# A graph attention layer on one core: later stores, counting before the unit, and another split of the slots

## The reference

```python
# x: 8192 x 256, adj: 8192 x 8192 f32, sparse: about 16 positive values a row, far more in the
# first rows; H = 8 heads of D = 32; W, Wr: 256 x 256
h0 = relu(layernorm(x))
h = (h0 @ W.T).reshape(n, 8, 32)
s_src, s_dst = einsum(h, a_src), einsum(h, a_dst)            # n x 8 each
attn = s_src[:, None, :] + s_dst[None, :, :] + adj[:, :, None] * We[:, 0] + be
attn = leaky_relu(where(adj[:, :, None] > 0, attn, -inf), 0.2)
attn = softmax(attn, axis=1)
out = x + einsum('ijh,jhd->ihd', attn, h) + h0 @ Wr.T + br
```

## Time and profile before

| | us |
|---|---|
| median of 3 runs | 2901.33 (2899.38 to 2902.26) |
| profiled execution | 2921.01 |
| its span | 2919.2 |
| VectorE busy | 2210.1 (76%) |
| POOL busy | 1471.8 (50%) |
| ScalarE busy | 1270.4 (44%) |
| TensorE busy | 1241.1 (43%) |
| gathers (L491) | 943 + 194, 1137 in all |
| activations that weight (L944) | 4024 |
| stores (L500) | 60 of 63 recorded, mean 1.644 |

### The profile page before, as it was taken

One profiled execution on the slowest core, in us unless ns is written; L12 is line 12 of the kernel. 1 busy time (PEld: TensorE's weight loads), 2 busy tenths in 40 slices (PEclk: granted clock), 3 DMA queues, 4 the chain that ended last, 5 costly groups with the idle time before them and its releaser, 6 DMA issues.

```text
span 2919.2 us, 27617 instructions
## 1 busy us (share of the span) xinstructions
PE 1241.1 (43%) x5305; PEld 934.9 (32%) x5306; DVE 2210.1 (76%) x5479; ACT 1270.4 (44%) x4898; POOL 1471.8 (50%) x1649
## 2 busy tenths in 40 slices
PE   7980040403351245523543351542352352436885
PEld 5650040303241133412332241332241241224664
DVE  3559879399997588668999798897998861129992
ACT  2320021102253278536845552743543563655663
POOL 5763655635736644565457647637537537530000
PEclk9995575756655566556656565656565666567998
DMA  3574647556666556656667668768758724257770
GB/s 119 190 283 147 181 134 222 87 198 168 200 187 195 172 173 177 175 150 208 202 203 233 206 193 231 227 183 228 215 183 229 216 62 98 70 162 165 197 156 3
DMA packets 226531, 512.82 MB, mean 176 GB/s; under 512 B 98280, under 2 KB 116400, under 8 KB 224208
## 3 DMA queue, kind: packets, MB, share of 16 engines
q1 hardware_dynamic: 151280, 319.60, 34.3%
q0 software_dynamic: 74960, 191.61, 26.4%
q10 hardware_dynamic: 144, 0.13, 0.0%
HBM read 475.19 MB, written 36.03 MB: 175 GB/s over the span
## 4 chain that ended last, share of the span: by engine, by line
issue 30%; DVE 22%; DMA 21%; PE 9%; ACT 7%; POOL 5%; another core or an unknown queue 2%; SPq 2%; DVEq 0%; POOLq 0%; ACTq 0%; PEldq 0%
DMA adj_sb<-in_adj_dram 16%; DVE work L617 6%; ACT arena L944 6%; DVE work L613 6%; POOL arena L491 4%; DMA arena<-table,arena 3%; DVE arena L753 2%; PE banks L1055 2%; PE banks L1049 2%; SPq L392 1%; DMA arena<-table,own 1%; PE banks L1098 1%; PE banks L1052 1%; DVE work L649 1%
## 5 line engine op out<-in xcount | busy, mean ns | idle before, releaser
L491 POOL DMA_INDIRECT arena<-table,arena x943 | 958.0, 1016 | 398.2 <-issue 281.2
L1076 PE MATMUL banks<-arena,ident 128*128 128x256 f32 x1268 | 421.0, 507 | 1326.6 <-DVE arena L753 1182.9
L944 ACT ACTIVATE arena<-arena,prob 128x32 f32<-128x32 f32 x4024 | 879.9, 316 | 107.7 <-issue 103.0
L1076 PEld LDWEIGHTS banks<-arena,ident 128*128 128x128 f32 x1268 | 326.0, 263 | 1418.9 <-issue 1080.3
L617 DVE FIND_INDEX8 work<-work,adj_sb 128x8 uint32<-128x176 f32 (+30 forms) x833 | 645.5, 799 | 1.0 <-issue 1.0
L613 DVE MAX8 work<-adj_sb 128x8 f32<-128x176 f32 (+30 forms) x833 | 594.2, 789 | 65.8 <-DMA adj_sb<-in_adj_dram 62.2
L939 ACT ACTIVATE prob<-pre 128x104 f32<-128x104 f32 (+26 forms) x63 | 20.3, 322 | 1058.3 <-DVE pre L737 704.6
L1082 PE MATMUL banks<-arena,ident 128*128 128x256 f32 x1006 | 321.7, 452 | 224.0 <-remote 118.4
L1082 PEld LDWEIGHTS banks<-arena,ident 128*128 128x128 f32 x1006 | 202.4, 218 | 332.3 <-remote 135.3
L491 POOL DMA_INDIRECT arena<-table,own x194 | 204.0, 1052 | 156.1 <-issue 62.9
L500 POOL DMA_INDIRECT out_dram<-w_all,arena x60 | 98.6, 1644 | 281.1 <-DVE w_all L763 220.9
(11 more groups left out here) (140 smaller groups left out, 1882.2 us busy)
## 6 DMA issues: line engine op xcount, KB each, us to landing
adj_sb<-in_adj_dram SPq DMA_DIRECT2D x504, 512.0 KB
arena<-dst_rows SPq DMA_DIRECT2D x16, 2048.0 KB, 8.8
arena<-table,arena POOLq DMA_INDIRECT x943
table<-arena POOLq DMA_DIRECT2D x32, 264.0 KB, 2.9
arena<-in_x_dram SPq DMA_DIRECT2D x32, 256.0 KB, 3.0
resid<-arena POOLq DMA_DIRECT2D x32, 256.0 KB, 2.6
out_dram<-arena POOLq DMA_DIRECT2D x32, 256.0 KB, 2.8
work<-table SPq DMA_DIRECT2D x8, 1024.0 KB, 11.2
```

What stands on the lines that cost most here:

```text
L491: pool.indirect_dma_start(gath[:, un.slot(k), :], None, table[:, :], bass.IndirectOffsetOnAxis(ap=rec[:, k, 0:1], axis=0), bounds_check=N ...
L944: last = s.activation(g, g, ACT.Copy, scale=prob[:, b, k * H + h:k * H + h + 1])
L1076: last = m.matmul(ps_sum[:, u % 2, :], ident[:, :], gath[:, un.slot(k), 0:HD], start=(k == 0), stop=False)
```

## The change

- POOL stores a unit's result six units later instead of three (LATE), for which there are eight output buffers instead of four (OUTS): four where they were, two in a spare part of the work memory, two new ones.
- The ring of gathered slots has 84 slots instead of 86.
- FOUND and LEAD: up to two finds more are done by the end of a unit.
- `act_slots`: a unit of fewer than 24 slots gives ScalarE all but two of them, and at most 13; before it was half of them below 18 slots, 10 for 18 and 19, and 14 for 20 to 23. Other units are as before.
- `placed_at` is gone. In the unit in which a group's last tile is found, all finds are done first, then the group is counted, then come the unit's softmax, weights and evacuation, and then place. TensorE does the group's ranks ahead of the unit's sums instead of behind them.

By the plan the groups are now counted and placed in units 1, 4, 8, 16, 24, 32, 40 and 48 and dealt after 2, 5, 12, 20, 28, 36, 44 and 52; the last find is in unit 48. ScalarE has 667 of the 1137 slots instead of 503: 12 more in units 10 to 15, 115 more in units 16 to 48 and 37 more (71 to 108) in units 49 to 62.

```diff
@@ -35,7 +35,7 @@
 PAD = 8
 JBITS = 17
 LOW = (1 << JBITS) - 1
-GSLOTS = 86
+GSLOTS = 84
 LANES = 4
 PIECES = 8
 PIECE = N // PIECES
@@ -53,16 +53,16 @@
           (56, (20, 13, 11, 10, 9, 8, 7, 6)))
 DIRECT = (75, 61, 58)
 SEGS = {1: (45, 2.2), 2: (30, 1.8), 3: (22, 1.8), 8: (18, 1.6), 14: (14, 1.8), 32: (9, 1.8)}
-FOUND = (4, 7, 10, 12, 15, 16, 18, 20, 21, 22)
-LEAD = 13
+FOUND = (4, 7, 10, 12, 15, 17, 19, 21, 23, 24)
+LEAD = 15
 GMAX = max(len(ks) for _, ks in GROUPS)
 KLIST = max(ks[0] for _, ks in GROUPS)
 KMAX = 8 * (max(DIRECT) // 8 + 1)
 VMAX = 8 * max(n for n, _ in SEGS.values())
 WIDE = max(len(ks) * (HEAD + 2 * ks[0]) for _, ks in GROUPS)
 RANKS = max(len(ks) * (ks[0] + 1) for _, ks in GROUPS)
-OUTS = 4
-LATE = 3
+OUTS = 8
+LATE = 6
 GROUP = 8
 HALF = N // 2
 
@@ -81,7 +81,7 @@
 
     def __init__(self, u, K, source, group, place):
         self.u, self.K, self.source, self.group, self.place = u, K, source, group, place
-        self.act_slots = K // 2 if K < 18 else 10 if K < 20 or K > 38 else 14 if K < 32 else 16
+        self.act_slots = min(K - 2, 13) if K < 24 else 10 if K > 38 else 14 if K < 32 else 16
         self.parts = 2 if K < 30 else 3 if K < 40 else 8
 
     def dve_parts(self):
@@ -122,8 +122,7 @@
     found = [FOUND[u] if u < len(FOUND) else min(len(sources), u + LEAD) for u in range(len(units))]
     for group in groups:
         group.ranked_at = min(u for u in range(len(units)) if found[u] >= group.listed)
-        group.placed_at = min(group.ranked_at + 1, group.first - 2)
-        group.dealt_after = min(max(group.placed_at + 1, group.first - 3), group.first - 1)
+        group.dealt_after = min(max(group.ranked_at + 1, group.first - 3), group.first - 1)
         group.loaded_after = min(group.dealt_after + 1, group.first - 1)
 
     at, owner, part_sums, acts, issued = 0, [None] * GSLOTS, 0, 0, 0
@@ -250,7 +249,9 @@
         rsum = sb("rsum", [P, H])
         rinv = sb("rinv", [P, 2, H])
         w_flat = w_all[:, :, :].rearrange("p c n -> p (c n)")
-        out_sb = w_flat[:, 0:OUTS * HD].rearrange("p (b n) -> p b n", n=HD)
+        out_more = sb("out_more", [P, 2, HD])
+        out_sb = [w_flat[:, i * HD:(i + 1) * HD] for i in range(4)] + [spare(HD) for i in range(2)]
+        out_sb += [out_more[:, i, :] for i in range(2)]
         pad_row = prob[0:PAD, 0, 0:ROW]
 
 
@@ -499,7 +500,7 @@
                 lane = turn(un.store_seq)
                 pool.indirect_dma_start(
                     out[:, :], bass.IndirectOffsetOnAxis(ap=record(un)[:, 0:1].bitcast(U32), axis=0),
-                    out_sb[:, un.u % OUTS, :], None,
+                    out_sb[un.u % OUTS], None,
                     bounds_check=N - 1, oob_is_err=False, compute_op=ALU.add).then_inc(lane, 16)
 
             def deal(group):
@@ -760,18 +761,21 @@
                 dve.wait_ge(S["recip"], u + 1)
                 if u >= OUTS:
                     landed(dve, units[u - OUTS].store_seq + 1)
-                v.tensor_tensor(out_sb[:, u % OUTS, :].rearrange("p (h d) -> p h d", d=D),
+                v.tensor_tensor(out_sb[u % OUTS].rearrange("p (h d) -> p h d", d=D),
                                 ps_sum[:, u % 2, :].rearrange("p (h d) -> p h d", d=D),
                                 rinv[:, u % 2, :].unsqueeze(2).to_broadcast([P, H, D]), ALU.mult).then_inc(S["evac"], 1)
 
             done_finds = 0
             for un in units:
-                while done_finds < found[un.u] - 1:
+                ranked = [group for group in groups if group.ranked_at == un.u]
+                while done_finds < found[un.u] - (not ranked):
                     find(done_finds)
                     for m in range(2 * sources[done_finds].rounds):
                         sort_step(done_finds, m)
                     decode(done_finds)
                     done_finds += 1
+                for group in ranked:
+                    count(group)
                 c = done_finds if done_finds < found[un.u] else None
                 steps = 0 if c is None else 2 * sources[c].rounds
                 if c is not None:
@@ -786,13 +790,8 @@
                     done_finds += 1
                 if un.u:
                     evacuate(units[un.u - 1])
-                for group in groups:
-                    if group.placed_at == un.u > group.ranked_at:
-                        place(group)
-                    if group.ranked_at == un.u:
-                        count(group)
-                        if group.placed_at == un.u:
-                            place(group)
+                for group in ranked:
+                    place(group)
             evacuate(units[-1])
 
             dve.wait_ge(S["fl_t"], 1)
@@ -1101,10 +1100,10 @@
                          ).then_inc(S["rank_ps"], 1)
 
             for un in units:
-                tile_sums(un)
                 for group in groups:
                     if group.ranked_at == un.u:
                         ranks(group)
+                tile_sums(un)
 
             pe.wait_ge(S["over_c"], len(groups))
             pe.wait_ge(S["flag_b"], TILES - FIRST)
```

## The result

The changed kernel takes 3012.15 us (3008.2 to 3013.05, four executions) against 2901.8 us (2899.38 to 2903.96) for the kernel before: a ratio of 1.0378 with a 95% interval of 1.036 to 1.0396. The forecast was 2872 us, its range 2820 to 2940. The changed kernel's profiled execution took 3012.46 us (span 3010.6), 91.5 us more than the 2921.01 of before; that execution of before was itself 19 us above its median.

What follows compares the result with a forecast made beforehand. Bounds taken: VectorE up to 1409 us (fully from 839), chained adjacency pieces to 2351, then ScalarE's weighting. Gains 44 + 50 = 94, losses 28 + 37 = 65, 29 us net: 2901 - 29 = 2872 us, range 2820 to 2940.

Steps and rivals of the forecast that it cites:

- A: Stretch until tile 32's load is issued, 1409 us before: 44 us gained, 94 with X.
- A, group 0's wait: VectorE's wait for TensorE's ranks before group 0's placement in unit 1: it goes, 45.2 us gained.
- A, the other placements and the finds: Up to tile 32's load: new rank waits lose 9 us, finds gain 8, slots gain 3, finds before softmax lose 3.
- X: VectorE's late short operations, 839 to 1409 us: 50 us gained of 126 idle; range 30 to 80, chance 0.38.
- the sign of X = 0: Tile 32's load issued near 1365 us instead of about 1315 would mean no late short operations gained.
- B: From tile 32's load until the last adjacency piece lands: chained pieces set the time, four rank waits lose 28 us.
- C: Tail after the last piece lands, 249 us before, bound by ScalarE's weighting: 22 us plus 15 of late activations, 37 lost.
- Costs nothing: Stores three units later and two ring slots fewer: no loss counted; of the last stores only 2 to 6 us could show.
- The second: Rival: ScalarE's tail and the later groups' rank waits decide, slower at 2944 us, extreme 2965; chance 0.24.
- Pieces didn't become slower: Rival: adjacency pieces of the chained stretch slow beside more gathers, 2910 us, up to 2920; chance 0.09.

Runs made afterwards that it cites:

- e8: Kernel before with at most two gathers outstanding instead of four, third chip: ratio 1.1535 to the kernel before.
- e6: Kernel before with only stores six units behind, eight output buffers and 84 ring slots, third chip: ratio 1.0255 to the kernel before.
- e13: Changed kernel, unchanged, on the fifth chip, which has no late starts: ratio 1.036 to the kernel before.
- e1: Changed kernel with place one unit after the count again (group 0 still in its own unit), second chip: 3057.07 us, ratio 1.0383 to the kernel before.
- e14: Kernel before, unchanged, traced on the fifth chip, which has no late starts: 2707.55 us.
- e15: Changed kernel with the old rule for ScalarE's slots, fifth chip: 2748.91 us, ratio 1.0163 to the kernel before.
- e17: Kernel before with only stores six units behind, eight buffers and 84 ring slots, sixth chip: ratio 1.0016 to the kernel before.

## Why the prediction was wrong

**A, group 0's wait: right.** The 45.2 us were there and went, and nothing took their place at once: VectorE begins the find behind the placement 35 us earlier (538.2 us, where it was 573.2). But their size was the first chip's. On the fifth the same wait was 17.5 us.

**A, the other placements and the finds: about right.** VectorE is 11 us less busy up to tile 32's load (946 against 957), which I had as 8 + 3. All placements there wait 20.2 us, where 57.8 us were before with group 0's; that is 37.6 gained against 36 forecast.

**X, the fallen step.** I took 50 us of late starts as gained because the stretch 225 to 839 had few of them. In all of A they fell by 8 us, from 145.4 to 137.3, and the waits for ScalarE's exponentials, which I had left out, took 13 back. So A gained 47 us rather than 94; tile 32's load at 1362 us is what I had put down as the sign of X = 0. The 43 us of idle time that I set against 126 also held 21.0 us of unit 0's rows. Late starts go with how long POOL issues without a pause (e8, and the sorting under e6) and with the chip (none on three of six). A difference between two stages of one trace was no ground for half of them to go; the later stores take pauses from POOL (its waits for VectorE at stores fell from 220.9 to 139 us here, and from 223.4 to 37 in e6), so the edit spoke against it. Without X my sum would have been 21 us of loss, so this step made the forecast a gain; B and C were too small besides, and with their measured 64 and 74 even an X of 50 would have left a loss.

**B: 64 for 28.** Two figures were off. The wait was 15 us a placement, not 11: I put 4.5 to 5 us of VectorE's work between count and place, and the new slots leave 3.2. And I set 4.5 us of slack against it. On the chip without late starts, four waits of 53.6 us in all cost 39, so 3.6 us a wait were absorbed, near the 4.5 set, and each wait of a placement is followed by one of SP's queue (48.0 us in all). The other 25 us on the first chip lie nearly all at the first of the four: SP's queue waits 36.8 us for VectorE there and 13.2 in e13. The placement waits 18.8 us there rather than 12.4, and late starts and others add 14 us between the same two finds. But e1 shows such a stretch, 1009 us, without any placement's wait, on a chip with late starts; how the placement and ScalarE's slots share B on such a chip stays open.

**C: 74 for 37.** The sum for the tail itself, 270.8 us, is near e13's 263. What it was set against was wrong. I had ScalarE as the bound of the kernel before's tail; the same sum with its 60 slots in twelve units gives about 162 us, and the tail took 249. POOL's gathers were most of its bound: e14 waits 108.4 us for gathered rows. So the extra slots first made ScalarE the bound. e15 prices this: 47 us for the slots (216 against 263), and nothing for two more units behind the last find (216 against e14's 221). Late starts are the rest: the first chip's tail after has 60 us more than e13's, and the one before 28 more than e14's; I had added 15.

**Costs nothing: wrong for the stores.** I saw the 220.9 us for which POOL waits at stores as an engine's idle time. On a chip with late starts the later stores cost 2.6% (e6); without them 0.2% (e17).

**The rivals.** The second, ScalarE's tail and the placements' waits, is what happened, and its 2944 us and even its 2965 were too small by the parts of B and C above. The forecast's chance of 0.38 rested on X alone. Pieces didn't become slower: where SP's queue doesn't wait for VectorE, issues of the chain in B lie 3.65 us apart on average before and 3.68 after.

## What to carry to other kernels

When two engines share work that a third thing already bounds (here a chain of transfers, and in the tail the gathers), moving it buys nothing, and it costs as soon as the engine that gets the work becomes the bound, so give such a rule its own value for each stage. Test a sum for a stage on the kernel before first: one that gives 162 us for a stage that took 249 has the wrong bound. A wait that is moved into the same unit as its cause has to be priced with the work that is then left between them, not with the work there before. And don't book as a gain idle time whose cause you haven't found: an engine's pause at a semaphore may be what keeps it from disturbing the others.

## What the runs showed of the hardware

Chips differ: the kernel before took 2708 to 2953 us on six of them. On three chips ScalarE's and VectorE's short instructions start late while POOL issues indirect gathers without a pause, one activation often by 1.1 us and in e1 by up to 1.8; on the other three chips every trace with 4024 weighting activations has 2.0 us of idle time before all of them. With at most two gathers outstanding the late starts were gone on a chip that has them (e8, 2.0 us). What makes a chip do this was not found.
